# A routed-attention and mixture-of-experts block on one core: attention block by block, and the work on finished batches stretched over the expert units

## The reference, cut to what matters

```python
h = _layernorm(x) * (1 + ca) + sa
x = x + ga * attn(h)             # below
h = _layernorm(x) * (1 + cb) + sb
x = x + gb * ffn(h)              # below

# attn: top 2 of 8 experts, rows sorted by expert, 256 at most of each expert and batch
q = (xe @ q_w) ; k = (xe @ k_w[e]) ; v = (xe @ v_w[e])
q = (q @ fmq1_w) * (q @ fmq2_w) ; k = (k @ fmk1_w) * (k @ fmk2_w)
attn = einsum('bihd,bjhd->bhij', qb, kb) * causal           # linear, no softmax
out = attn @ v + qb @ state ; state = state + kb^T @ vb
out = (restored * rw).sum(2)                                # two rows of each token
out = out * rsqrt(mean(out * out) + EPS) * norm_w ; out = out @ o_w

# ffn
h = x @ lin0_w + lin0_b ; h = silu(h @ w1 + b1) * (h @ w2 + b2)
scores = softmax(h @ gate_w.T) ; topv, topi = top_k(scores, 4) ; normalised
yexp = (silu(h @ exp_w1[e]) * (h @ exp_w3[e])) @ exp_w2[e]  # 8 experts, 2 shared
h = lin1 and swiglu of (sum of combine * yexp + shared)
```

## Time and profile before

| | us |
|---|---|
| median of 3 runs | 1449.04 (1444.19 to 1450.4) |
| the profiled execution, whole | 1450.58 |
| its span, first to last instruction | 1448.8 |
| stage one, to the first key product of attention | 213 |
| attention, to the end of the last block | 653 (213 to 866) |
| last steps of batches, and the part between | 171.5 (866 to 1037.5, the first `ep`) |
| expert units and the last tail | 411 (1037.5 to 1448.8) |

### The profile page before, as it was taken

One profiled execution on the slowest core, in us unless ns is written; L12 is line 12 of the kernel. 1 busy time (PEld: TensorE's weight loads), 2 busy tenths in 40 slices (PEclk: granted clock), 3 DMA queues, 4 the chain that ended last, 5 costly groups with the idle time before them and its releaser, 6 DMA issues. The chain is left out here.

```text
span 1448.8 us, 27085 instructions
## 1 busy us (share of the span) xinstructions
PE 1127.1 (78%) x9330; PEld 802.7 (55%) x9330; DVE 875.1 (60%) x1823; ACT 683.7 (47%) x1653; POOL 586.2 (40%) x626
## 2 busy tenths in 40 slices
PE   2891118889877888888898885663699999999997
PEld 2671006666655565555666652321477777777774
DVE  5447275666456666665777767325366666666664
ACT  1460004555445565555666653332355555555553
POOL 1003403442555445554333335503245454545541
PEclk8895559999898999999999995555699999999997
DMA  9921112332332222222222111100432332424220
GB/s 310 390 113 47 69 48 77 103 90 78 97 89 83 72 79 87 84 84 66 71 58 67 56 35 29 27 3 0 123 107 83 96 101 78 118 66 131 66 73 14
DMA packets 83536, 125.71 MB, mean 87 GB/s; under 512 B 9041, under 2 KB 65873, under 8 KB 79313
## 3 DMA queue, kind: packets, MB, share of 16 engines
q1 hardware_dynamic: 73168, 98.86, 22.6%
q0 software_dynamic: 10240, 25.18, 5.4%
HBM read 71.32 MB, written 52.69 MB: 86 GB/s over the span
## 5 line engine op out<-in xcount | busy, mean ns | idle before, releaser
L1142 DVE SCALAR_TENSOR_TENSOR att<-reach,endrel,wide 128x1024 f32<-128x1024 f32 x160 | 204.4, 1277 | 197.0 <-PE wide L995 146.1
L1437 POOL TENSOR_TENSOR eg<-eg,hq 128x512 f32<-128x512 f32 x128 | 172.7, 1355 | 211.6 <-ACT eg L1532 183.4
L1561 DVE TENSOR_TENSOR epp<-ep,epp 128x512 fp32r<-128x512 f32 x160 | 148.9, 930 | 131.4 <-ACT epp L1537 129.9
L199 POOL DMA_INDIRECT routed_rows<-hq,idxs x128 | 132.5, 1035 | 189.3 <-DVEq L611 117.3
L756 POOL TENSOR_TENSOR sm<-su,headm 128x128 f32<-128x128 f32 x160 | 76.2, 476 | 289.4 <-DVE su L1154 287.7
L978 PE MATMUL bank<-kvw,turned 128*128 x320 | 148.9, 547 | 32.8 <-DVE kf L1136 25.3
L1481 PE MATMUL bank<-epp,w2p 128*128 128x512 f32 x480 | 156.4, 434 | 2.9 <-DVE epp L1561 2.9
L1537 ACT ACTIVATE epp<-ep 128x512 fp32r<-128x512 f32 x160 | 100.8, 630 | 104.9 <-DVE ep L1568 104.9
L765 POOL DMA_INDIRECT gst<-attended_rows,idxs x128 | 133.5, 1043 | 33.5 <-issue 32.8
L850 ACT ACTIVATE k1s<-bank 128x128 f32<-128x128 f32 x160 | 44.4, 278 | 181.7 <-PE bank L978 173.4
L995 PE MATMUL wide<-turned,kx 32*128 32x128 f32 x2560 | 108.9, 291 | 5.9 <-ACT kx L864 3.6
(11 more groups left out here) (269 smaller groups left out, 2166.2 us busy)
## 6 DMA issues: line engine op xcount, KB each, us to landing
hq<-weight_rows SPq DMA_DIRECT2D x16, 2048.0 KB, 9.7
routed_rows<-zero SPq DMA_DIRECT2D x4, 5120.0 KB, 24.5
rows<-routed_rows SPq DMA_DIRECT2D x80, 256.0 KB
attended_rows<-ob SPq DMA_DIRECT2D x80, 128.0 KB
out<-fin SPq DMA_DIRECT2D x16, 256.0 KB, 2.5
routed_rows<-hq,idxs POOLq DMA_INDIRECT x128
gst<-attended_rows,idxs POOLq DMA_INDIRECT x128
kw_raw<-in_k_w SPq DMA_DIRECT2D x1, 512.0 KB, 5.3
```

Of the source, the lines that this page charges most:

```text
L199: pool.indirect_dma_start(hs[s], bass.IndirectOffsetOnAxis(idxs[:, t, k:k + 1], 0), hq[:, t, :], None, bounds_check=BLOCKS[s] * P - 1, oob ...
L1142: dve.scalar_tensor_tensor(out=att[:, n % 2, :, :], in0=reach[:, :, :].rearrange("p a c -> p (a c)").unsqueeze(1) .to_broadcast([P, 4, 2 * ...
L1437: pool.tensor_tensor(g, g, rows_of(b % 2, n, n + 1), ALU.mult).then_inc(s_eu, 1)
L1561: dve.tensor_tensor(epp[:, (k - 1) % RING, 1, :], ep[:, (k - 1) % RING, :], epp[:, (k - 1) % RING, 0, :], ALU.subtract).then_inc(s_el, 1)
```

## The change

Four edits.

1. **Attention by single blocks.** The loop goes over blocks n from -6 to 159, no longer pairs. Scores and attending are done for one block at a time, on one half of the PSUM tile `wide`. Key products run 5 blocks ahead instead of 2, rows are turned 3 pairs ahead. Masking the state moves from POOL (L756) to DVE, which masks both states of a pair in one instruction (`mask_states`) ahead of the running sum. Several tiles are deeper (`vx` 6, `turned` 3, `kf`, `km` 4), `rows` has 3 buffers instead of 4, and `kf`, `km`, `qm`, `sm` lie in the first 16 tiles of `hq`.
2. **Steps that run on.** J1[b] is now 86 + 10 b (C0[1] is 40). The steps are functions `post_pool`, `post_act`, `post_pe`, `post_freed` and `post_dve` that both loops call: attention for slots up to 159, and the expert units for slot 160 + k. The loop after the last block is gone. The sum of the two gathered rows moves from POOL to DVE; the weighting on ACT is in two halves.
3. **Router in groups of four.** The choices are made for four batches at once in 11 parts in successive slots (33 small DVE instructions of 128 columns, an Exp on ACT, four transposes, one store), four times in all. In the expert units fall groups 1, 2 and 3, beginning in units 13, 53 and 93.
4. **Weights split in stage one.** ACT makes the three high parts in the middle of the loop of stage one and POOL the low parts; ACT waits for POOL ahead of step 12, because the raw weights now lie in the last tiles of `hq`.

In the expert units the Silu's input has 2 PSUM banks instead of 3, since bank 3 stays with the steps.

```diff
-            def steps(eng, step):
+            def steps(eng, step, halfway=None, late=None):
...
+                def split_weights():
+                    act.wait_ge(s_w1, 16 * NW1)
+                    for w, parts in ((w1s, w1p), (w3s, w3p), (w2s, w2p)):
+                        act.activation(parts[:, 0, :, :], w[:, :, :], ACT.Copy).then_inc(s_wh, 1)
+
+                steps(act, step, split_weights, lambda: act.wait_ge(s_wl, 3))
...
-        PERIOD, GATHER = 10, 16
+        PERIOD, GATHER, CHAIN, ROUTE = 10, 19, 10, 33
+        J1 = [C0[1] + 46 + PERIOD * b for b in range(NB)]
...
-                for g in ITERATIONS:
-                    if here(g + 1):
-                        keys_values(2 * g + 2)
-                    if here(g + 2):
-                        turn(g + 2)
-                    if here(g):
-                        states(g)
...
-                    post(2 * g)
-                    post(2 * g + 1)
-                    if here(g):
-                        carried(g)
...
-                    if here(g):
-                        attend(g)
-                    if here(g + 1):
-                        scores(g + 1)
+                for n in ITERATIONS:
+                    h, odd = divmod(n, 2)
+                    if is_block(n + 1):
+                        scores(n + 1)
+                    if is_block(n):
+                        attend(n)
+                    if not odd and here(h + 1):
+                        states(h + 1, n)
+                    if is_block(n + 5):
+                        keys_values(n + 5)
...
+                    post_pe(pe, n)
+                    if is_block(n + 1):
+                        carried(n + 1)
...
+                for n in ITERATIONS:
+                    h, odd = divmod(n, 2)
+                    if is_block(n + 1):
+                        mask_scores(n + 1)
+                    if not odd and here(h + 1):
+                        mask_states(h + 1)
+                    if is_block(n + 2):
+                        mask_q(n + 2)
+                    if is_block(n + 5):
+                        k_features(n + 5)
+                    if is_block(n + 2):
+                        sum_state(n + 2)
+                    post_freed(dve, n)
+                    post_dve(dve, n)
...
                     if b < NB:
                         up(k)
+                    post_pe(pe, NBK + k)
                     if b:
                         tail(b - 1, n)
...
+                    post_act(act, NBK + k)
...
                 for k in range(UNITS + NU):
                     b, n = divmod(k, NU)
+                    post_freed(dve, NBK + k)
                     if b:
                         tail(b - 1, n)
...
+                    post_dve(dve, NBK + k)
```

More of the change, by code:

```diff
@@ new lines, in adaln_block @@
+        oTs = tb("oTs", [P, 2 * P])
+        ob = tb("ob", [P, 2, 2, D])
+        s_ld = [sem(f"rows_loaded{i}") for i in range(3)]
+        s_t = sem("rows_turned")
+        s_te = sem("turned_copied")
+        s_kv = sem("k_v_products")
+        s_ve = sem("k1_v_copied")
+        s_vz = sem("zeros_between")
+        s_kf = sem("k_features")
+        s_km = sem("k_features_masked")
+        s_kt = sem("k_turned")
+        s_kx = sem("k_heads_split")
+        s_qm = sem("q_masked")
+        s_s = sem("scores_ready")
@@ new lines, in adaln_block, with here, is_block, _ @@
+        s_a = sem("scores_masked")
+        s_st = sem("states_ready")
+        s_sh = sem("states_masked")
+        s_sm = sem("states_summed")
+        s_o = sem("attended")
+        s_oc = sem("attended_copied")
+        s_ot = sem("attended_turned")
+        s_oe = sem("attended_rows_ready")
+        def here(g):
+            return 0 <= g < PAIRS
+        def is_block(n):
+            return 0 <= n < NBK
+        ITERATIONS = range(-6, NBK)
+        with nc.Block() as block:
+            @block.gpsimd
+            def _(pool):
+                sent = [NT * TOPA * B0[1]]
+                def scatters(n):
@@ new lines, in _ @@
+                for n in ITERATIONS:
+                    h, odd = divmod(n, 2)
[7 more added lines that the diff above has]
+                        keys_values(n + 5)
+                    if not odd and here(h + 3):
+                        turn(h + 3)
+                    if odd and here(h):
+                        turn_outputs(h)
+                    if odd and here(h + 2):
+                        turn_k(h + 2)
+                    if not odd and here(h + 1):
+                        pe.wait_ge(s_sh, h + 2)
+                    post_pe(pe, n)
+                    if is_block(n + 1):
+                        carried(n + 1)
@@ L1429, in _ @@
             def _(pool):
+                for b in range(2):
+                    hidden_parts(pool, b, b)
                 for k in range(UNITS):
@@ L1531, in _ @@
                         act.wait_ge(s_eg, k + 1)
[L1532 removed]
+                        act.activation(eg[:, k % RING, :], gate_bank[k % 2][:, :], ACT.Silu).then_inc(s_es, 1)
                     if 1 <= k <= UNITS:
```

1030 lines of the change are left out of this document (482 added, 548 removed).

## The result

The changed kernel took 1491.9 us (median of 4 runs, 1489.8 to 1495.8) where the kernel before took 1448.7: a ratio of 1.031, 95% interval 1.027 to 1.034. It is slower by 3.1%. The forecast was 1301, with a range of 1230 to 1365 and 4% for slower.

What follows compares the result with a forecast made beforehand. It took PE as the bound in attention without steps (some 10% idle) and in the units, with nothing covering the stretch between. Terms: 1450.6 + 6 - 81 - 159.5 + 85 = 1301 us, range 1230 to 1365.

Steps and rivals of the forecast that it cites:

- (a): Stage one: splitting the weights there on ACT and POOL adds 6 us, between 0 and 13.
- (b): Attention, first block to last: 77 blocks at 3.1 us, 83 at 3.85, plus 13 for filling; 572 against 653, -81.
- (c): Bare stretch between attention and first `ep`: steps, splitting, choices and DRAM trip go, 12 us stay; -159.5.
- (d): Expert units: steps moved there add 54 for PE, 16 for ACT, 9 for tables, 6 for DVE; +85.
- the third rival: Units: POOL's SBUF reads hold up DVE's step instructions at the port; 42 more, 1343 us; chance 0.12.
- the fifth rival: Units: PE is not fed, idling 1.16 us at each of a batch's 28 step instructions; 1593 us; chance 0.04.

Runs made afterwards that it cites:

- after: The changed kernel as first measured and profiled, against the kernel before: 1491.9 us, ratio 1.031.
- e1: Changed kernel with POOL waiting in each attention slot on ACT's key and value products, so scatters and gathers go out one a slot: 1369.3 us, ratio 0.945.
- f1: The changed kernel itself, run again on another chip where the kernel before took 1362.4 us: 1282.8 us, ratio 0.941.
- f3: Kernel before with one memset behind each of the first 32 scatters in stage one, on f1's chip: 1381.9 us, ratio 1.015.
- e9: e1 with the last two super-batches' scatters spread evenly and one memset behind each of stage one's first 32 scatters: 1299.2 us; kernel before there 1357.6.
- f2: The kernel of e9 again, on f1's chip: 1299.7 us, ratio 0.954 to the kernel before.
- e12: e1 with gathers from the third batch on as plain DMAs of 128 rows in order, on e9's chip: 1272.5 us.
- f4: The kernel of e7 again, on f1's chip: 1284.1 us.
- e7: e1 plus a burst of 32 indirect DMAs of 16 bytes a row in slot 27, nobody waiting for them: 1409.7 us.
- g2: The kernel of e9 again, on a chip where the kernel before took 1447 us: 1354.0 us, ratio 0.935.
- e6: e1 with a small tile filled twice behind each of the first 32 scatters in stage one: 1367.5 us.
- e2: Changed kernel without e1's wait, but with three memsets, each waited for, behind each scatter of attention: 1387.0 us.
- e4: e1 with the 32 scatters of each super-batch sent in one burst: 1453.9 us.

## Why the prediction was wrong

Each term in us, forecast and measured by the profiled spans (kernel before: 1448.8). Borders are the first turning of rows, the end of the last attending and the first `ep`:

| term | forecast | after | paced (e1) | f1 against the earlier trace rows | f1 against f3 |
|---|---|---|---|---|---|
| (a) stage one | +6 | +4 | +6 | -25 | +8 |
| (b) attention | -81 | +84 | -42 | -97 | -42 |
| (c) between | -159.5 | -155 | -154 | -152 | -152 |
| (d) units | +85 | +107 | +112 | +109 | +109 |
| sum | -149.5 | +39 | -78 | -166 | -78 |

f1 ran on a chip without the stall and the earlier trace rows come from one with it, so the fourth column mixes the change with the chip. The last one compares like with like: f3 is the kernel before on f1's chip, with the spacing in stage one. Its attention took 600 us, the stretch between 171 and the units 411.5, the last two as in the earlier trace rows. The +8 is an estimate, from f3's first turning at 198.5 us, f1's at 186.7, and the 19.5 us by which f3 is longer than the kernel before. So the change without its pacing fault is worth 78 to 80 us on either kind of chip, about half of what was forecast.

**What bounds the kernel.** Half right. The bare 171 us, and PE as the bound of the units, hold. But the PE idle time of attention was put down to waiting in turn, and part was the stall: on a chip without it the old attention takes 600 us (f3), not 655, its blocks 40 to 60 3.52 each instead of 4.33. Those blocks have scatters and gathers; I had read the 4.36 as the price of the steps.

**(a)** right: first key product at 217 (after) and 219 (e1), forecast 219.

**(b)** is the step that failed, twice. First, the pacing. The prediction counts it for the change that it "takes POOL's last arithmetic away", and costs only the work that moves to DVE. I asked who waits for POOL, not for what POOL waits; what its scatters would do with nothing to hold them back stands in no term. Of "after"'s 739 us, 181 go with the stall (558 in f1), and one wait gives 125 of them back. Second, the gain itself. In f1 attention takes 558 us, even below the forecast of 572; its blocks take 3.0 up to the 77th (3.1 forecast) and 3.8 on the mean behind it (3.85). That step of the working was sound. But the old side of the difference, 653, held about 55 us of stall: without it the gain is 600 - 558 = 42, not 81. And where there is the stall, pacing doesn't take all of it away: e1's attention takes 613 us against 557 for the paced kernels e9 and f2. That price of one scatter a block is in no term either.

**(c)** right but for some us: 15.8 to 18.5 left, 12 forecast. The load of the router's weights lands 10 us after its issue, as forecast, but it is issued only 4.5 (after) to 7.3 us (f1) behind the last attending, for which the term had nothing.

**(d)** mis-sized by 22 to 27. PE's added work was right: a ten of units with steps has 29.9 us of it against 24.3 without. The first two rows here are tens of e1 with a router's parts and without them, the third has no steps (windows, columns of the earlier trace rows):

```profile
881.00:921.30 40.30, 36.35 (x140) 25.62 (x139) 34.62 (x74) 25.13 (x46) 24.05 (x21) 0.92 0.24 66
1137.50:1169.10 31.60, 29.86 (x119) 21.93 (x118) 22.60 (x41) 17.26 (x31) 12.56 (x10) 0.95 0.27 76
1255.00:1279.90 24.90, 24.27 (x101) 18.35 (x100) 16.61 (x24) 13.44 (x24) 13.02 (x11) 1.00 0.34 97
```

By the starts of `ep` the first ten tens of e1 took 33.4, 40.3, 37.0, 34.5, 35.0, 40.3, 37.0, 32.3, 31.6 and 33.5 us. So the plain ones are within the forecast 32 to 34, or just over. The four that hold parts of the router's second and third group exceed it by 3 to 6 each, 19 in sum (the last group falls on the last steps), where I had 6 for DVE in all. In the longest DVE is busy 34.6 of 40.3. Part of that is the port, the third rival in small. One step instruction in f1, in attention and then in the units, and another (first group of each pair in attention):

```profile
L897 DVE SCALAR_TENSOR_TENSOR tmp<-tmp,var 128x36 f32<-128x36 f32 x21 | 4.1, 196 | 0.7
...
L897 DVE SCALAR_TENSOR_TENSOR tmp<-tmp,var 128x36 f32<-128x36 f32 x24 | 11.7, 486 | 0.8
...
L991 DVE TENSOR_TENSOR gst<-gst,inv 128x512 f32<-128x512 f32 x8 | 5.5, 684 | 0.0
...
L991 DVE TENSOR_TENSOR gst<-gst,inv 128x512 f32<-128x512 f32 x8 | 8.9, 1118 | 0.0
```

0.20 became 0.49 us and 0.68 became 1.12 where POOL has its product beside them. My argument against the third rival, that the steps come behind `ep` when POOL is done, doesn't hold. The Trainium skill (SBUF — State Buffer, Who interferes with whom) says that a DVE instruction with two inputs in SBUF and a GpSimd instruction that reads SBUF exclude each other; these rows agree. That this makes the missing 22 us, rather than the handovers, was not tried. With plain gathers (e12) the units took 510 us, with indirect ones on the same chip (e9) 518, so some 8 us more hang on the gathers. The granted clock in e1's ten tens with steps was 0.93 on the mean (0.85 to 1.00), not 1.0, and PE was busy 82 to 94% of each, where I had said over 90.

**The rivals.** The fifth came nearest: PE idle with nothing that it waits for, with the very row of stage one. I gave it 4% and placed it in the units, where the steps are, at a price for each instruction. The stops came in attention and behind POOL's bursts. The argument against it, that attention in the trace of before shows nothing of the kind, was weak, since there the scatters were paced, and wrong by the 55 us above. The question "what made those 1.16 us?" had an answer in the trace: POOL's first 32 scatters ran beside them. The Trainium skill (Runtime: NRT & Kernel Launch, Instruction fetch mechanics) has the fetching hidden behind the running page. f4 agrees (PE busy 27.1 of 28 us). e7 (0 of 27) would contradict it only if that stop were one of fetching, and the queue rows of 328 to 375 us speak against that. I had read this page as ruling the fifth rival out; it rules out one cause of such idle time, not the idle time.

**The time of 1301** is 18 us from what the change takes on the second kind of chip, and that is luck. The kernel before takes 1362 there, some 86 us less than the forecast started from, and the change gains 80 there, some 70 less than forecast. The two errors nearly cancel.

## What to carry to other kernels

When a change takes an engine's work away, look for the waits that go with it: the work may have been the only thing that paced what is queued behind it, DMAs above all. Pace indirect DMAs by the consumer's progress, one for each step of the work, even where nobody needs them late. A stretch in which an engine idles on "issue" wants a cause before its price is put anywhere: look at what else is being sent there. Few instruction packets in such a stretch prove nothing by themselves; see whether one has to land before the engine goes on. And time the kernel before beside the new one on every chip: the change alone took 1492 on one and 1283 on another.

## What the runs showed of the hardware

- On at least three chips of five or six, indirect DMAs sent by POOL every 1.28 us slow PE, DVE and ACT at once and all but stop them after some 12 us, until the burst ends (28 us lost for a burst of 41, 6.7 for one of 10). 16 bytes a row do the same; plain DMAs of the full size, in a burst of 17 us, do not. On two chips nothing of this happens (f1 and f4 on one, e9 and e12 on the other).
- Spacing at 2.1 (g2) to 2.5 us (e6) is enough to end the stall in stage one, and 3.14 us (e2) the long stops in attention. A price stays: with a scatter a block (3.2 us apart, e1) a block takes 3.25 on the first kind, against 3.0 without scatters ("after", blocks 20 to 40) and against 3.0 with them on the second (e9).
- PE's granted clock was 0.50, the lower level of 1.2 GHz, in the holes of "after", e4 and e7, in which it stood idle, and was at 0.72 on the mean in the 17 us behind the hole of e4.
- What differs between the chips stays open: the instruction packets themselves took about 1.0 us in "after" and 1.1 in f1 (median of queue 8), and nothing in the traces names the cause. Nor is it known how the bursts stop the engines. The expectations took it for late refills; in e7 PE went on without one.
